# Six small moves in the instruction order of a fused decoder layer: key loads on ScalarE's queue, four VectorE steps and two conversions

## What is computed

```python
x = layernorm(x + self_attention(x))      # 16 heads of 128; weights are 4-bit codes times a scale per 32 rows
x = layernorm(x + cross_attention(x, ctx_2048))   # 1,024 context rows as keys and values, the 54 largest scores of a row
x = layernorm(x + ffn(x))                 # silu(x @ Wg.T) * (x @ Wu.T) @ Wd.T, 2,048 wide
```

## Time and profile before

| | |
|---|---|
| median of three runs | 911.99 us (911.7 to 912.0) |
| profiled execution | 911.83 us, of which the span from first to last instruction is 910.0 us |
| mean granted TensorE clock | 0.999 |
| TensorE busy | 900.3 us (99%), weight loads 747.6 us (82%) |
| VectorE, ScalarE, GpSimd busy | 588.6 us (65%), 582.6 us (64%), 498.5 us (55%) |
| DMA | 76.97 MB, mean 85 GB/s |

### The profile page before, as it was taken

The page is one execution under the profiler, slowest core; times in us unless marked ns, Lnnn a source line. Parts: engine busy times, 40 slices in busy tenths (PEclk is TensorE's granted clock), DMA queues, the critical chain, the costliest instruction groups (busy, mean ns, idle before and its releaser), DMA issues.

```text
span 910.0 us, 13246 instructions
## 1 busy us (share of the span) xinstructions
PE 900.3 (99%) x4440; PEld 747.6 (82%) x4440; DVE 588.6 (65%) x1057; ACT 582.6 (64%) x1161; POOL 498.5 (55%) x413
## 2 busy tenths in 40 slices
PE   9999999999999999999999999999999999999997
PEld 7888788888888888888778888998888888888885
DVE  5767966678667687676696999987797125511114
ACT  5667976688767788678875686634656535533333
POOL 4258742656515576477784677726574833345540
PEclk9999999999999999999999999999999999999999
DMA  6531330122300322222131213423433431333321
GB/s 209 163 106 57 90 91 1 44 80 76 91 15 30 94 76 58 66 78 74 47 115 47 71 48 96 125 70 114 129 110 96 121 92 55 122 113 104 90 74 46
DMA packets 46102, 76.97 MB, mean 85 GB/s; under 512 B 5584, under 2 KB 11216, under 8 KB 45776
## 3 DMA queue, kind: packets, MB, share of 16 engines
q1 hardware_dynamic: 45888, 76.00, 28.6%
q10 hardware_dynamic: 144, 0.07, 0.0%
HBM read 73.69 MB, written 2.36 MB: 84 GB/s over the span
## 4 chain that ended last, share of the span: by engine, by line
PE 86%; DVE 8%; issue 2%; ACT 1%; POOL 1%; DMA 0%; SPq 0%; DVEq 0%; POOLq 0%; ACTq 0%
PE p L1004 6%; PE p L1008 6%; PE p L1005 6%; PE p L746 6%; PE p L783 5%; PE p L748 4%; PE p L728 3%; PE p L1018 3%; PE p L724 3%; PE p L1019 3%; PE p L1020 3%; PE p L726 3%; PE p L793 3%; PE p L797 3%; PE p L794 3%; PE p L768 3%
## 5 line engine op out<-in xcount | busy, mean ns | idle before, releaser
L2172 POOL TENSOR_TENSOR V<-RAW,V 128x512 fp32r<-128x512 f32 x64 | 81.7, 1299 | 129.7 <-ACT V L1190 129.7
L1658 DVE TENSOR_SCALAR_CACHE_REDUCE JK<-p,ssc 128x512 bf16<-128x512 f32 x112 | 83.6, 747 | 98.4 <-PE p L728 98.3
L1131 ACT ACTIVATE PR<-p,nms,ssc 128x512 f32<-128x512 f32 x112 | 87.3, 780 | 59.5 <-DVE JK L1658 58.7
L2167 POOL TENSOR_TENSOR acc<-SX,acc 128x512 f32<-128x512 f32 x56 | 72.8, 1300 | 60.1 <-ACT SX L1170 34.9
L746 PE MATMUL p<-R 128*128 128x512 f32 x248 | 97.3, 392 | 0.1
L2172 POOL TENSOR_TENSOR C<-RAW,C 128x512 fp32r<-128x512 f32 x58 | 76.8, 1333 | 27.9 <-ACT C L1190 27.8
L1671 DVE TENSOR_TENSOR PT<-p,PT 128x512 fp32r<-128x512 f32 x128 | 87.3, 682 | 3.0 <-ACT PT L1150 2.9
L2001 DVE TENSOR_TENSOR SX<-p,SX 128x512 f32<-128x512 f32 x32 | 22.0, 689 | 99.8 <-PE p L1008 90.5
L783 PEld LDWEIGHTS p<-ident,PR 128*128 128x128 f32 x512 | 63.5, 140 | 17.2 <-DVE PT L1671 0.9
L783 PE MATMUL p<-ident,PR 128*128 128x128 f32 x512 | 76.7, 272 | 0.2 <-ACT PR L1131 0.2
L1150 ACT ACTIVATE PT<-p 128x512 fp32r<-128x512 f32 x128 | 75.9, 593 | 0.0
(11 more groups left out here) (251 smaller groups left out, 2716.4 us busy)
## 6 DMA issues: line engine op xcount, KB each, us to landing
RAW<-in_wg SPq DMA_DIRECT2D x32, 256.0 KB, 2.9
RAW<-in_wu SPq DMA_DIRECT2D x32, 256.0 KB, 2.6
RAW<-in_ctxn SPq DMA_DIRECT2D x32, 256.0 KB, 2.8
RAW<-in_wd SPq DMA_DIRECT2D x32, 256.0 KB, 2.8
RAW<-in_wq SPq DMA_DIRECT2D x19, 256.0 KB, 2.6
RAW<-in_wk SPq DMA_DIRECT2D x19, 256.0 KB, 2.7
RAW<-in_wv SPq DMA_DIRECT2D x16, 256.0 KB, 3.4
RAW<-in_wo SPq DMA_DIRECT2D x16, 256.0 KB, 3.3
```

The lines of the kernel that those rows point to most:

```text
L1131: e.activation(PR[:, i % 2, :], P[i % 2][:, :], ACT.Exp, bias=nms[:, i % 4:i % 4 + 1], scale=ssc[:, 0:1] if HB[j][0] > 1 else SC, accum_ou ...
L1658: e.tensor_scalar(JK[:, :], P[i % 2][:, :], ssc[:, 1:2] if HB[i // 4][0] > 1 else -SC, None, ALU.mult, ALU.min, accum_out=nms[:, i % 4:i % ...
L2172: e.tensor_tensor(lo, RAW[:, slot[key], :], hi, ALU.subtract).then_inc(*c_lo.up(key))
```

## The change

Key loads go from SyncE's queue to ScalarE's, behind the query scales, and VectorE takes the query's low half before the key's multiply. The value bias of the fourth piece of the output weight is added at the end of VectorE's step i = 16 instead of at its beginning. At i = 121 the key's low half comes before the maximum. The first norm reciprocal comes before one search step, which is done after the second. ScalarE makes conversions 8 and 9 after the copies of tile 2 together with conversion 10, and GpSimd subtracts their low halves after those of tile 2.

```diff
@@ sync
             load_raw(("qk", 0, 0), wq[0])
-            e.dma_start(SCL[:, 1, 0:128], blocks8(sk, 0)).then_inc(*k_scl_in.up())
-            e.dma_start(RAW[:, 1, :], wk[0]).then_inc(*k_raw_in.up())
             slot["qk", 0, 1], in_slot[1] = 1, ("qk", 0, 1)
@@ scalar
             e.dma_start(SCL[:, 0, 0:128], blocks8(sq, 0)).then_inc(*q_scl_in.up())
+            e.dma_start(SCL[:, 1, 0:128], blocks8(sk, 0)).then_inc(*k_scl_in.up())
+            e.dma_start(RAW[:, 1, :], wk[0]).then_inc(*k_raw_in.up())
@@ scalar, cross-attention
             search(topk.run(4))
-            conv_cn(2)
             search(topk.until(0))
...
                 px_high(2, hf, 6 + hf)
-            conv_cn()
+            conv_cn(3)
@@ vector, start
             multiply(("qk", 0, 0))
+            low(("qk", 0, 0))
             multiply(("qk", 0, 1))
-            low(("qk", 0, 0))
             x_low(0, 0)
@@ vector, self-attention
-                if qt == 0 and i > 4:
+                if qt == 0 and i > 16:
                     for piece in pieces_at(i - 1):
                         if piece[0] == "o":
                             value_bias(piece)
...
+                if i == 121:
+                    qk_low(j + 1, qt)
                 if i + 2 < 4 * NJ:
                     maximum(i + 2)
-                if qt < 2 and j + 1 < NJ:
+                if qt < 2 and j + 1 < NJ and i != 121:
                     qk_low(j + 1, qt)
...
                 factor(i)
-                if qt or i == 4:
+                if qt or i in (4, 16):
                     for piece in pieces_at(i - 1):
                         if piece[0] == "o":
                             value_bias(piece)
@@ vector, cross-attention
             ln_stats(1, [4, 5], (15, 1))
-            search(topk.run(1))
             ln_bias(4)
             search(topk.run(1))
             ln_stats(1, [6, 7], (15, 1))
             ln_bias(6)
-            search(topk.run(6))
+            search(topk.run(7))
@@ gpsimd
                     px_low(n, hf)
-            conv_cn(3 + 3 + 2)
+            conv_cn(3 + 3)
             for hf in range(2):
                 px_low(2, hf)
-            conv_cn(3 + 3)
+            conv_cn(2 + 3 + 3)
```

## The result

The changed kernel took 917.19 us, the median of four runs (915.52, 916.88, 917.50 and 917.94), beside 911.85 us for the kernel before (four runs, 911.43 to 912.00). The ratio is 1.0055, with an interval of 1.0043 to 1.0068: slower by 0.55%, 5.3 us, where 911.7 us was forecast, with a range of 910.3 to 912.6. The profiled execution is the fastest of the four, 915.52 us with a span of 913.7.

What follows compares the result with a forecast made beforehand. TensorE, 99% busy, was taken as the bound, so only its stops count. Start +0.1, value bias 0, i = 121 -0.35, norm and conversions +0.1 sum to -0.15 us: 911.83 becomes 911.7, range 910.3 to 912.6.

Steps and rivals of the forecast that it cites:

- The start: Key scales and weight on ScalarE's queue, VectorE's query low half ahead of the key multiply: forecast +0.1 us.
- T - 6.75: Worth in us of moving the key loads: the weight's new arrival less the arrival that leaves TensorE's 8.86 us unchanged.
- T: New arrival time of the key weight at the kernel's beginning, not in the trace; taken as 6.85 us.
- rival 3: Slower: key weight shares DMA engines with x and small scale pieces; two x pieces ahead give 912.6 us; chance 0.13.
- one x piece ahead or at half rate beside the weight: Price of DMA competition for the key weight: 0.8 us per 256 KB, so arrival at 7.0 us.
- the trough also gives time back: Reason for taking arrival 6.85 us: x can fill the slow early DMA stretch left by small scale pieces.
- The sign that the prediction gave for itself: Key weight arriving after 7.3 us would show the forecast for the moved loads wrong.
- needs T near 9 or an effect not seen: Condition for a result over 913.8 us, slower by over 0.2%; chance 0.03.
- The value bias: VectorE, i = 16: bias starts at 91.7, takes 1.55 us beside GpSimd; worth 0, bounds -0.75 and +0.2 us.
- i = 121: Key's low half before the maximum removes TensorE's stop at 474.65 us: -0.35 us, between 0 and -0.5.
- an output tile and eight transposes: TensorE's own next work after 474.65 us, said to hide VectorE low halves moved by 0.33 us.
- Norm and conversions: One sum: stops at 524 and 581 us go, a GpSimd wait at 584 replaces them; +0.1 us, bounds -1.25 and +0.4.

Runs made afterwards that it cites:

- the start alone: The kernel before with only the two key loads moved to ScalarE's queue and VectorE's new order at the beginning: 914.92 us, ratio 1.0035.
- the later edits alone: The kernel before with value bias, key half at i = 121, norm reciprocal and conversions changed, loads and first VectorE order as before: 912.72 us, ratio 1.0008.
- the conversions alone: The kernel before with only ScalarE's conversions 8 and 9 put behind the copies of tile 2: 912.18 us, ratio 1.0002.

## Why the prediction was wrong

**The start: the step that failed.** The frame held: the edit is worth T - 6.75. With T = 9.28 that is 2.53 us, and the 19 weight loads start at 11.41 instead of 8.86 us, 2.55 later; with the start alone T was 9.80, which gives 3.05, and they start at 11.94, 3.08 later. (The chain from T to the key's low half was put at 2.09 us and measured 2.07.) What was wrong is T, taken as 6.85, with 7.8 as the far end in rival 3. I priced the competition as "one x piece ahead or at half rate beside the weight", for the weight alone. The scales ahead of it on the same ring share with x too, in the first microseconds about a small packet for a large one. The sum by the windows of the two traces, an account and not a test: 0.74 MB moved from 3.4 us to the weight's multiply at 6.2 before, 1.54 MB from 3.4 to 9.3 us after. The 0.8 MB between them are as much as three x pieces, 2.5 us at the 322 GB/s of the earlier trace rows. The lower rate of the first 2.8 us costs 0.28 MB, 0.9 us more, and a higher one later gives some 0.3 back: 3.1 us, which is 9.28 - 6.20. The sentence "the trough also gives time back" had the wrong sign: with both rings at work the trough got longer.

The Trainium skill's rule beside rival 3 (DMA: Bandwidth & Descriptors, 🔬 Queues, rings and completion order: each DMA engine takes turns between the queues, a packet each) was the one to follow. The trace agrees in kind for the first stretch, 183 packets beside 145, and not for the next, 354 beside 166; whether the trace's packets are the page's is not shown. The rule was applied to the weight alone, not to the scales ahead of it. The sign that the prediction gave for itself, a key weight later than 7.3 us, is what came.

**The clock: a step that was missing.** I wrote that over 913.8 "needs T near 9 or an effect not seen"; it was both. The longer stop costs its own length, and in three of the changed kernel's four executions a stretch at the low clock behind it. The earlier trace rows showed a stop of 1.0 us with no such price, and the text never asked what a longer one would cost. It is 1.7 us in the median: 917.19 less the 915.52 of the one execution with the clock at 0.999, on top of the trace's 3.7.

**The value bias: right.** Start forecast 91.7, measured 91.79 alone; length taken 1.55, measured 1.51; worth 0. The Trainium skill's port rule (SBUF — State Buffer, 🔬 SBUF: two separate sides) says that one of the two blocks the other. By it the prediction put the bias's end half a microsecond after that of GpSimd's multiply, and the trace agrees: 93.30 against 92.75.

**i = 121: the gain right, its cover wrong.** Forecast -0.35; the runs' trace shows the stop gone and a new one of 0.60 us. The prediction named "an output tile and eight transposes" as what hides VectorE's delay, but not the bank that the next output tile needs. Net +0.33 in all three traces that have the edit (0.20 to 0.53 late alone, 0.34 to 0.67 with the later edits, 2.68 to 3.01 in the changed kernel) instead of -0.35. The bounds, 0 to -0.5, left out a loss.

**Norm and conversions: right up to 587 us, and a term missing behind it.** The stop at 524 went: 0.46 us won and 0.15 more between the two rows' transposes, as forecast (0.65), but 0.29 of it was given back at the next transposes (530.67). The copies ran where the sum had them, and the wait for GpSimd's conversion 8 came where it was named: by 587.29 the pair had cost 0.2 us (3.20 less the 3.01 ahead of it), against +0.1 forecast. What the sum left out is where VectorE's chain of searches is paid. It became some 0.9 us later at first (its next step at 530.53 instead of 526.64, less TensorE's 3.0; forecast 0.7, but the last row's statistics also waited 0.26 us for GpSimd) and was still 0.5 later at 576 us. The prediction followed it to ScalarE's copies and dropped it there. But VectorE goes on with it to the low halves that TensorE needs at 598.30, for which the kernel before has no wait and no room either: there TensorE's lateness becomes VectorE's, 3.68 us in the changed kernel, 1.5 with the later edits alone, 0.76 with the conversions alone. That costs the last 0.5 us, and the pair comes to 0.7 (3.68 less 3.01); the upper bound was 0.4. What a gain ahead of it can win at most is therefore set by this chain.

Summed up, the later edits were forecast at -0.25 and came to about +1.1 in the trace and +0.7 in the runs. The start was forecast at +0.1 and came to 2.55 us and, with the clock, to 4.2 in the changed kernel's median. 2.55 + 1.1 + 1.7 is the 5.3 us measured.

## What to carry to other kernels

A load moved to another engine's queue is not only issued at another time: here it left one order and entered a share with everything that ran beside its whole ring, the small pieces ahead of it included, and came 3.1 us later for an issue 0.2 us later. Before moving the load that the start waits for, count the packets on both rings up to it, not the bytes of the load alone. And where no idle time shows in front of an instruction, compare its start with the end of what releases it: 0.06 us of distance, as at 477.10, means no cover. Follow an engine whose queue runs back to back to the next place where the bottleneck needs it, not only to the next visible stop.

## What was not expected of the hardware

- With two rings at work on small and large packets the total fell to 95 to 113 GB/s in the four slices from 3.5 to 4.9 us, where the kernel before had 86, 202, 294 and 316, while the engines were as busy (90% against 91% of their time from 3.4 to 6.2 us). Why a packet on SyncE's ring then takes twice as long was not tried.
- TensorE's clock fell to half at 10.77 us, during a stop of 2.8 us, and came back after 3.41 us; three of the changed kernel's four runs carry the mark of it in their mean (0.996 to 0.997). In its profiled execution, with a stop of 2.0 us, and in that of the start alone, with 2.5, there was none.
- Nine matmuls that nobody reads, 2.17 us of work, made a kernel some 2 us faster.
